# Centring the experts' first projections once, dropping the layers' centred copy, and taking the mean from a router column

## The reference

```python
def _moe_layer(x, rw, rb, g, b, w1, b1, w2, b2):
    logits = jnp.einsum('bsh,he->bse', x, rw) + rb
    probs = jax.nn.softmax(logits, axis=-1)
    vals, idx = jax.lax.top_k(probs, K)            # K = 2 of E = 4
    vals = vals / vals.sum(axis=-1, keepdims=True)
    mu = x.mean(axis=-1, keepdims=True)
    xc = x - mu
    xhat = xc * jax.lax.rsqrt((xc * xc).mean(axis=-1, keepdims=True) + EPS)
    xe = xhat[None] * g[:, None, None, :] + b[:, None, None, :]
    h = jax.nn.gelu(jnp.einsum('ebsh,ehf->ebsf', xe, w1) + b1[:, None, None, :], approximate=False)
    y = jnp.einsum('ebsf,efh->ebsh', h, w2) + b2[:, None, None, :]
    expert_out = x[None] + y
    comb = jnp.einsum('bsk,bske->bse', vals, jax.nn.one_hot(idx, E, dtype=x.dtype))
    return jnp.einsum('bse,ebsh->bsh', comb, expert_out)
x = hidden_states
for l in range(L):                                 # L = 4
    x = _moe_layer(x, router_w[l], router_b[l], ln_g[l], ln_b[l], w1[l], b1[l], w2[l], b2[l])
```

## Time and profile before

| | |
|---|---|
| median of 3 runs | 3143.62 us (3141.18 to 3147.69) |
| the profiled execution's own time | 3143.73 us |
| its span | 3141.7 us |
| PE busy | 2537.0 us, 81% of the span |
| DVE busy | 1943.4 us, 62% |
| ACT busy | 1386.7 us, 44% |
| POOL busy | 1062.8 us, 34% |
| mean granted clock of TensorE | 0.80 |

### The profile page before, as it was taken

The page is one execution under the profiler, slowest core; times in us unless marked ns, Lnnn a source line. Parts: engine busy times, 40 slices in busy tenths (PEclk is TensorE's granted clock), DMA queues, the critical chain, the costliest instruction groups (busy, mean ns, idle before and its releaser), DMA issues.

```text
span 3141.7 us, 30770 instructions
## 1 busy us (share of the span) xinstructions
PE 2537.0 (81%) x7208; PEld 1271.2 (40%) x7208; DVE 1943.4 (62%) x6569; ACT 1386.7 (44%) x4620; POOL 1062.8 (34%) x913
## 2 busy tenths in 40 slices
PE   4776884479996989789886998788978997889598
PEld 1122443244444444344444443444444444444344
DVE  4857587357775777567766677577766555444422
ACT  3232433435544555445544554445534444444233
POOL 4735257104542445235432455244422001100200
PEclk7587655659996899878996899789978996788699
DMA  3231332003321233113220332122311220111021
GB/s 108 68 84 54 89 99 72 25 13 100 101 66 28 80 96 90 42 46 101 78 71 27 92 97 75 25 73 84 92 33 46 65 64 21 34 64 58 10 81 57
DMA packets 111774, 204.70 MB, mean 65 GB/s; under 512 B 14799, under 2 KB 24422, under 8 KB 111592
## 3 DMA queue, kind: packets, MB, share of 16 engines
q1 hardware_dynamic: 111592, 202.75, 22.1%
HBM read 195.36 MB, written 7.34 MB: 65 GB/s over the span
## 4 chain that ended last, share of the span: by engine, by line
PE 41%; DVE 28%; ACT 14%; issue 7%; POOL 1%; DVEq 0%; POOLq 0%; ACTq 0%
PE p_hid L656 8%; DVE state L1197 7%; PE p_turn L905 7%; PE p_misc L666 4%; ACT cell_t L919 4%; DVE cell L935 3%; DVE add_c L932 3%; PE p_acc L666 3%; DVE weighed L1206 2%; DVE p_turn L929 2%; PE p_misc L354 2%; PE p_gate L465 2%; DVE hist L940 2%; PE p_turn L475 1%; ACT cand L916 1%
## 5 line engine op out<-in xcount | busy, mean ns | idle before, releaser
L905 PEld LDWEIGHTS p_turn<-hist,w_hh 22*128 22x128 f32 x2048 | 371.6, 225 | 1148.2 <-DVE hist L940 1013.9
L905 PE MATMUL p_turn<-hist,w_hh 22*128 22x4 f32 x2048 | 457.3, 291 | 420.2 <-DVE hist L940 402.2
L656 PE MATMUL p_hid<-xhat,w 128*128 128x512 f32 x1024 | 581.8, 652 | 1.1 <-ACT hid L714 0.7
L919 ACT ACTIVATE cell_t<-cell 20x4 f32<-20x4 f32 x1024 | 207.7, 203 | 701.7 <-DVE cell L935 701.7
L1135 POOL TENSOR_TENSOR drive<-du,rows 128x512 f32<-128x512 f32 x256 | 473.4, 1849 | 63.2 <-DVE state L1197 44.9
L929 DVE SCALAR_TENSOR_TENSOR p_turn<-p_turn,cell 20x4 f32<-20x4 f32 x1024 | 170.7, 167 | 500.8 <-ACT p_turn L915 478.9
L714 ACT ACTIVATE hid<-p_hid,b1f 128x512 f32<-128x512 f32 x512 | 351.6, 687 | 243.1 <-PE p_misc L666 151.1
L388 POOL TENSOR_TENSOR n_rstd<-n_var,minus_half 128x4 f32<-128x4 f32 x56 | 62.0, 1108 | 1098.3 <-DVE n_var L376 1098.3
L1197 DVE TENSOR_TENSOR_SCAN state<-decay,drive 128x512 f32<-128x512 f32 x256 | 398.1, 1555 | 25.2 <-POOL drive L1139 15.7
L1154 POOL TENSOR_TENSOR y<-y,weighed 128x512 f32<-128x512 f32 x192 | 242.4, 1262 | 450.5 <-DVE weighed L1206 449.9
L940 DVE SCALAR_TENSOR_TENSOR hist<-p_turn,cell_t 20x4 f32<-20x4 f32 x1024 | 162.7, 159 | 275.6 <-ACT cell_t L919 275.6
(11 more groups left out here) (204 smaller groups left out, 3161.5 us busy)
## 6 DMA issues: line engine op xcount, KB each, us to landing
rows<-rows_dram SPq DMA_DIRECT2D x128, 512.0 KB, 5.0
w<-w_dram SPq DMA_DIRECT2D x128, 256.0 KB, 2.7
w<-in_w2T SPq DMA_DIRECT2D x128, 256.0 KB, 2.7
comb_b<-comb_dram SPq DMA_DIRECT2D x64, 512.0 KB, 4.7
rows<-comb_dram SPq DMA_DIRECT2D x128, 128.0 KB, 2.9
w<-in_w1T SPq DMA_DIRECT2D x16, 256.0 KB, 2.8
w_dram<-w SPq DMA_DIRECT2D x16, 256.0 KB, 2.4
out_xT<-result SPq DMA_DIRECT2D x8, 256.0 KB, 2.5
```

The costliest lines, as they stand in the source:

```text
L656: nc.tensor.matmul(p_hid[:, v % 2, :], w1[:, v // FB, (v % FB) * P:(v % FB + 1) * P], xhat[:, :], start=True, stop=True).then_inc(g_h, 1)
L905: nc.tensor.matmul(gate_bank(i)[:, :, t:t + 1], w_hh[:, :], before, start=False, stop=False, skip_group_check=True).then_inc(gates_done, 1)
L919: nc.scalar.activation(cell_t[64:64 + PE_, :], cell[32:32 + PE_, :], ACT.Tanh, scale=0.5).then_inc(cell_tanh, 1)
```

## The change

In the MoE layers the centred copy is gone. The router's matrix has a fifth column of 1/128, so that the mean of each token comes out of the logits' matmul; DVE copies it (`mean1`), squares it, and subtracts the square when it reads the sum of squares. ACT squares the layer's input itself, one slot earlier. `xhat` is input times scale. The projections are centred once in `fold`: behind the scaling by ln_g comes a matmul with the matrix of 1/128 over w1 and a subtraction. A layer has 22 slots in place of 23 (norm slots o = 0 to 3, first projection at o = 4, heavy slots 5 <= o < 21); the 8 decays stand in o = 21, 0, 1 and 2, two each. The period keeps its 128 slots, so its tail begins 4 slots earlier. The last norm behind the four layers stays as it was.

```diff
-    w_router1 = sbuf("w_router1", [P, L * E1])
+    w_router1 = sbuf("w_router1", [P, L, E1 + 1])
+    mean1 = sbuf("mean1", [P, B])
...
-    LAYER = UN + 7
+    NORM = 4
+    LAYER = NORM + UN + 2
...
@@ layer1_pe @@
-            ln = norm_pe(n1, q * NL + l, src, (n1.src_ready, q * NL + l + 1), logits, (lambda: mean_of_two(n)) if l else None)
-            for s_ in range(5):
-                next(ln)
-                if s_ == 4:
-                    pe.wait_ge(g_comb, n + 1)
...
-                yield
+            pe.wait_ge(n1.src_ready, q * NL + l + 1)
+            for j in range(B):
+                mm = nc.tensor.matmul(p_hid[:, 0, j * (E1 + 1):(j + 1) * (E1 + 1)], tile(src, j), w_router1[:, l, :],
+                                      start=True, stop=True)
+            mm.then_inc(g_logit, 1)
+            yield
+            pe.wait_ge(n1.square_done, q * NL + l + 1)
+            for j in range(B):
+                mm = nc.tensor.matmul(p_acc1[:, 448 + j:449 + j], tile(n1.square, j), mean_w[:, 0:1], start=True, stop=True)
+            mm.then_inc(n1.var_done, 1)
+            yield
+            yield
+            pe.wait_ge(n1.rstd_done, q * NL + l + 1)
...
@@ layer1_act @@
+            act.wait_ge(n1.src_ready, q * NL + l + 1)
+            if l:
+                act.wait_ge(n1.var_done, q * NL + l)
+            nc.scalar.activation(n1.square[:, :], src, ACT.Square).then_inc(n1.square_done, 1)
+            yield
+            choose_act(n, arg1, tanh1, g_arg, g_tanh)
+            yield
+            yield
...
@@ layer1_dve @@
+            next(ch)
+            nc.vector.tensor_copy(mean1[:, :], p_hid[:, 0, 0:B * (E1 + 1)].rearrange("p (b e) -> p b e", b=B)[:, :, E1:E1 + 1]
+                                  .rearrange("p b o -> p (b o)")).then_inc(mean_step, 1)
+            yield
+            next(ch)
+            dve.wait_ge(mean_step, 2 * n + 1)
+            nc.vector.tensor_tensor(mean1[:, :], mean1[:, :], mean1[:, :], ALU.mult).then_inc(mean_step, 1)
+            dve.wait_ge(mean_step, 2 * n + 2)
+            dve.wait_ge(n1.var_done, q * NL + l + 1)
+            nc.vector.scalar_tensor_tensor(out=n1.var[:, :], in0=p_acc1[:, 448:448 + B], scalar=EPS, in1=mean1[:, :],
+                                           op0=ALU.add, op1=ALU.subtract).then_inc(n1.var_taken, 1)
+            yield
+            next(ch)
+            next(ch, None)
+            yield
+            dve.wait_ge(n1.rstd_rows, q * NL + l + 1)
+            nc.vector.tensor_tensor(xhat[:, :], src, p_misc1[:, :], ALU.mult).then_inc(n1.out_done, 1)
+            yield
...
@@ fold_pe @@
             for _ in range(2):
                 yield
+            pe.wait_ge(fold_grown, k + 1)
+            if k:
+                pe.wait_ge(fold_scaled, k)
+            nc.tensor.matmul(p_misc1[:, :], mean_w[:, :], w1[:, k % E1, :], start=True, stop=True).then_inc(fold_mean, 1)
...
@@ fold_dve @@
+            dve.wait_ge(fold_mean, k + 1)
+            nc.vector.tensor_tensor(w1[:, k % E1, :], w1[:, k % E1, :], p_misc1[:, :], ALU.subtract).then_inc(fold_scaled, 1)
...
@@ period @@
-            heavy = layer1 is not None and slot >= att and 6 <= o < LAYER - 1 and slot < tail
+            heavy = layer1 is not None and slot >= att and NORM + 1 <= o < LAYER - 1 and slot < tail
...
-                    for _ in range({22: 1, 0: 2, 1: 2, 2: 2, 3: 1}.get(o, 0)):
+                    for _ in range({LAYER - 1: 2, 0: 2, 1: 2, 2: 2}.get(o, 0)):
```

More of the change, by code:

```diff
@@ L379, in norm_dve @@
         dve.wait_ge(nm.rstd_rows, n + 1)
-        dve.wait_ge(nm.centred_done, n + 1)
+        dve.wait_ge(nm.centred_done, (n + 1) if means is None else means)
         nc.vector.tensor_tensor(dst, nm.centred[:, :], nm.misc[:, :], ALU.mult).then_inc(nm.out_done, 1)
@@ L884, in layer1_pool @@
             yield
-        for l in range(L + 1):
-            yield from norm_pool(n1, q * NL + l)
-            for _ in range(LAYER - 5):
+        for l in range(L):
+            yield
+            pool.wait_ge(n1.var_taken, q * NL + l + 1)
+            nc.gpsimd.tensor_tensor(n1.rstd[:, :], n1.var[:, :], minus_half[:, :], ALU.pow).then_inc(n1.rstd_done, 1)
+            for _ in range(LAYER - 1):
                 yield
+        yield from norm_pool(n1, q * NL + L)
     def layer0_pool(q):
```

87 lines of the change are left out of this document (40 added, 47 removed).

## The result

The changed kernel takes 3176.58 us (median of 4 runs, 3162.69 to 3185.53) against 3142.4 us before: a ratio of 1.0106, 95% interval 1.0082 to 1.013. By the ratio it is 33 us slower; 3141 was forecast and the range ended at 3162. The profiled execution's own time is 3175.91 us, its span 3174.1 (before 3143.73 and 3141.7), the mean granted clock 0.77 (before 0.80).

A forecast was written before the change was run, and what follows sets the result against it. No one engine bounds the kernel; the slot is the unit, with a floor of 1.83 us set by the bare LSTM chain. Terms -12 - 5 - 3 + 17 = -3 us gave 3141 us, range 3118 to 3162.

The forecast's parts named there:

- Part 1, the starts: Starts of 20 layers, periods 1 to 5: 48.5 us shorter; -12 us net once returned slots are counted.
- One stretch more at the lower level: Layers' starts, periods 1 to 7: without mean matmuls TensorE stays slow longer, about 1 us a layer, up to +26; chance 0.12.
- the term of +0.5 us: Slot 0 of a layer's start: ACT's square ahead of its two decays makes the layer reach the spread 0.5 us later.
- Part 1, the returned slot: Period's tail, periods 1 to 5: each removed slot comes back at the floor of 1.83 us or a little more.
- Part 2, soft: Borders of periods: 4 more of `soft`'s slots run in the empty end of a period, out of the attention; -5 us.
- Part 3: Periods 6, 7 and 8: little changes in the layers' starts; -3 us in sum (-8 to +3).
- Part 4, the fold: `fold` in period 0: 16 added matmuls and 16 subtractions cost 1.1 us each, +17 us (+10 to +32).
- The wait in every second fold slot: Sign for period 0: DVE's subtraction waits for PE in every second fold slot, period 0 longer by 17 us.
- The sum: Whole kernel: -12 - 5 - 3 + 17 = -3 us, giving 3141 us, no difference that a measurement can tell.
- the clock: Rival, layers' starts of periods 1 to 7: lower clock without mean matmuls, 3167 us, half of it 3154; chance 0.12.
- the wait in `fold`: Rival, `fold`: each subtraction waits for its matmul at the lower level, +32 there, 3159 us in all; chance 0.18.
- a granted clock below 0.84 in periods 1 to 5: Sign named ahead as speaking for the clock rival, chance 0.12.

The follow-up runs named there:

- e3: e2 with a layer's 23 slots kept (one more norm slot); 3149.9 us, ratio 1.0058 to the kernel before.
- e4: e2 with the mean matmuls done again where they stood, read by nobody; 3137.81 us, ratio 1.0013 to the kernel before.
- e2: The changed kernel without the centring in fold, the layers' part alone; 3155.28 us, ratio 1.0071 to the kernel before.
- e1: The kernel before with only the centring in fold added; 3174.75 us, ratio 1.0128 to the kernel before.
- e5: e2 with leave, pre and soft held back by 4 slots; 3142.69 us, ratio 1.0012 to the kernel before.
- e11: e10 with the centring in fold added; 3156.45 us, ratio 1.0062 to the kernel before.
- e10: e2 with both repairs, the unread mean matmuls of e4 and the later leave and pre of e5; 3136.8 us, ratio 1.0002 to the kernel before.
- e6b: The kernel before with only the fold's 16 subtractions on DVE, read by nobody; 3157.05 us, ratio 1.0062 to the kernel before.
- e7: The kernel before with only the fold's 16 mean matmuls, read by nobody; 3146.58 us, ratio 1.0023 to the kernel before.
- e13: The kernel before with a delay of 8 unread DVE operations at the end of fold; 3158.25 us, ratio 1.0063 to the kernel before.
- e16: e2 with a delay of 8 unread DVE operations at the end of fold; 3158.32 us, ratio 1.0046 to the kernel before.
- e14: The kernel before with a delay of 4 unread DVE operations at the end of fold; 3146.43 us, ratio 0.9994 to the kernel before.

## Why the prediction was wrong

By its own steps:
- **Part 1, the starts: right in sign, 15 us too large.** The step that failed is that the removed matmuls were priced at a clock that stays as it was: as a gain of 8.5 us in 5 layers and nothing in the others. Taking them away costs 0.58%, 18 us, in both pairs of kernels that show it (before to e3, e4 to e2; in the second 14.6 us of it stand in the starts of 20 layers, 0.7 us each), and the clock in the starts falls from 0.80 before to 0.65 after. "One stretch more at the lower level" stood among the rivals with 0.12 and +1 us a layer. The rule that the prediction cited from the Trainium skill, page "TensorE: Matmul & The Clock Gate", section "What's actually happening", that the throttled state is the default and activity releases it, agrees as to the sign: the granted clock fell from 0.87 to 0.79 in period 2. What it doesn't tell is why PE stayed throttled with 12.30 of 12.30 us busy; no run here shows that. The chain on ACT in slot 0, on which the term of +0.5 us rested, is there in 14 of the 20 starts and absent in 6 at the lower level. The row that the forecast read it from doesn't show it in the kernel before: with the `[0.18 <-PE p_turn L905]` of the earlier trace rows, `L915` waited for PE there, not for the decays.
- **Part 1, the returned slot: the other failed step.** 1.83 us was read from slots without `layer0`. Attention and tail are 22 us longer than forecast, the largest single miss, and it has three parts: 4.5 us stand in e3 too, which returns no slot; 12.2 come with the slots (e3 to e2, 43.8 in place of 31.6, or 2.2 us a slot with soft's share in it); 5.5 come with the fold (e2 to after), which costs them 12.3 us where no slot is returned (e1). So of the (538.3 - 484.5) / 20 = 2.7 us that one would read from the changed kernel, not all is the slot's.
- **Part 2, soft: small, as taken.** Forecast -5; e5, which undoes it, doesn't lose by it (attention + tail 2.2 us less).
- **Part 3: forecast -3, measured -0.6**, period 6 being 3.7 longer at a clock of 0.84 in place of 0.88, period 8 2.3 shorter.
- **Part 4, the fold: right in period 0, where the forecast ended.** Forecast +17; period 0 is +12.9 in the changed kernel, +14.4 in e1, +13.8 in e11 (+17.5 against e10). The wait in every second fold slot, which was named as the sign, came: 10 of 16, 10.3 us. DVE's share was put too high, at 0.75 us each, 12 us; the subtraction alone costs 6.5 (e6b) and the matmul alone 6.7 (e7). What the forecast hadn't is a cost beyond period 0: e1 loses 40 us in all, e11 against e10 19. Where that comes from stays open.
- **The sum**: -33 in place of -48.5 (starts), +54 in place of +31.6 (attention and tail); every other term of the forecast is within about 4 us.

The rival "the clock" had the mechanism and 3154 to 3167; the measured time lies beyond it since attention and tail failed too. The rival "the wait in `fold`" added +32 for the fold to -9 for part 1 without saying why not -12; with -12 it was 3156. The sign "a granted clock below 0.84 in periods 1 to 5" was named ahead and came.

What stays open: the clock is not an input that a run can set, so that "the clock fell in another slot" is read from the traces behind e13 to e16 and not switched on and off. The mean matmuls, which hold the clock up in the starts, are switched on and off (e4 against e2); why a delay costs 20 us in one kernel and nothing in another, and with it the fold's cost beyond period 0, is not explained. Nor is it shown which of the two repairs works by which share: e5 changes the tail and wins 4 us in the starts and 6 in periods 6 and 7, in stretches whose instructions it leaves alone, and that is the same kind of shift. The executions of one kernel also scatter by 0.9% (before, 28 executions beside e14 to e16: 3130.82 to 3158.17 us), and the opening, which the layers' part and the delays leave alone, ends between 324.7 and 328.2 us. So one profiled execution tells a difference of a period only where it is large or comes again.

## What to carry to other kernels

Before a slot, a loop turn or a stage is priced at its floor, list everything that rides in it: what shared the removed slot moves with it, and the floor must be read from slots that still carry it. Here removed and returned slots came out even. When PE is busy in a stretch at the lower level, work removed from it isn't a gain of its duration: read the granted clock before and behind the removed matmuls, and price the slots behind them at both levels. And try a pure delay in the unchanged kernel before a loss of 0.5% is explained by what a change does: here one of 8 operations was worth 20 us, and one of 4, which left period 0 as late, nothing. Where such noise is as large as the effect, vary both parts of a change in a square and look for a quantity that parts all kernels, as the clock in the starts did.
